# Forget sums and token counts kept on VectorE's side in the first pass of a gated two-layer kernel

## The reference

```python
log_f = log_sigmoid(fg)                       # per head
cs = concat([0, cumsum(log_f)])
log_d = where(tri, (cs - cs.T)[1:, 1:] + ig.T, neg)
m = max(log_d, axis=-1)
d = exp(log_d - m)
c = q @ (k.T / sqrt(dh)) * d
n = maximum(sum(c), exp(-m))
h = c / (n + eps) @ v
...
idx = argmax(softmax(x @ wg))                 # one expert of 8 for each token
mask1 = one_hot(idx)
locations1 = cumsum(mask1, axis=0) - 1.0      # a token's place in its expert's queue
```

## Time and profile before

| what | value |
|---|---|
| median of three runs | 575.7 us (573.4 to 580.27) |
| the profiled execution | 577.31 us, its span 575.5 us |
| so outside the span | 1.8 us |
| first pass | about 0 to 285 us of the span |
| from the gate products at 50.68 us to those at 228.75 us | 12 steps, 14.8 us each on average |
| mean granted clock of TensorE over the span | 0.848 |

### The profile page before, as it was taken

The page is one execution under the profiler, slowest core; times in us unless marked ns, Lnnn a source line. Parts: engine busy times, 40 slices in busy tenths (PEclk is TensorE's granted clock), DMA queues, the critical chain, the costliest instruction groups (busy, mean ns, idle before and its releaser), DMA issues. The chain is left out here.

```text
span 575.5 us, 12773 instructions
## 1 busy us (share of the span) xinstructions
PE 478.4 (83%) x3787; PEld 358.4 (62%) x3787; DVE 333.2 (58%) x1455; ACT 306.5 (53%) x764; POOL 217.1 (38%) x210
## 2 busy tenths in 40 slices
PE   3589999999999999964469999999905788888884
PEld 2567787887877778843327777777702455665652
DVE  6335778877778777796322223333213667788772
ACT  4667666656566656331123333333204678888872
POOL 4301124434444435456500000000058888888400
PEclk9997778777787777795569999999965999999997
DMA  4973112222222111141122443343142556666531
GB/s 120 211 197 92 57 57 75 76 75 74 74 75 74 55 54 38 29 122 37 38 55 56 110 111 110 110 109 93 38 113 34 111 109 145 142 137 139 132 93 36
DMA packets 85067, 51.98 MB, mean 90 GB/s; under 512 B 7555, under 2 KB 78886, under 8 KB 85030
## 3 DMA queue, kind: packets, MB, share of 16 engines
q1 hardware_dynamic: 73766, 43.09, 27.3%
q0 software_dynamic: 11264, 8.43, 8.6%
HBM read 26.07 MB, written 16.91 MB: 75 GB/s over the span
## 5 line engine op out<-in xcount | busy, mean ns | idle before, releaser
L684 POOL DMA_INDIRECT s_xs<-slots_y,s_gidx x64 | 98.8, 1544 | 153.8 <-DMA slots_y<-s_ye 134.6
L814 ACT ACTIVATE s_ht<-heads,s_cols 128x512 f32<-128x512 f32 x64 | 44.0, 687 | 85.0 <-PE heads L1061 84.7
L147 ACT ACTIVATE s_xn<-s_xs,s_ln_shift,s_ln_rstd 128x128 f32 (+1 forms) x192 | 77.6, 481 | 15.6 <-DVE s_ln_shift L140 15.5
L662 POOL DMA_INDIRECT slots_x<-s_xn,s_sidx x64 | 62.8, 982 | 22.9 <-issue 22.9
L99 DVE BATCH_NORM_STATS2 s_ln_stats<-s_xs 128x6 f32 (+1 forms) x256 | 54.5, 279 | 25.8 <-DMA s_xs<-slots_y,s_gidx 20.3
L1061 PE MATMUL heads<-s_xet,s_w_sb 128*128 128x512 f32 x128 | 60.2, 615 | 1.7 <-DVE s_xet L1433 1.7
L1068 PE MATMUL bank<-s_w_sb,s_ht 128*128 128x128 f32 x512 | 59.9, 276 | 0.9 <-DVE s_ye L1442 0.9
L1068 PEld LDWEIGHTS bank<-s_w_sb,s_ht 128*128 128x128 f32 x512 | 58.5, 192 | 1.5 <-issue 1.5
L648 POOL TENSOR_TENSOR s_hs<-s_hs,s_head_w 128x512 f32<-128x512 f32 x16 | 20.3, 1268 | 95.0 <-DVE s_hs L1314 94.9
L960 PE MATMUL heads<-s_dec_r,s_dec_l 128*128 128x512 f32 x64 | 50.6, 938 | 2.0 <-DMA s_dec_r<-s_mrow 2.0
L985 PE MATMUL heads<-s_vaug,s_cw 64*64 64x33 f32 x1024 | 50.1, 270 | 0.1
(11 more groups left out here) (190 smaller groups left out, 934.5 us busy)
## 6 DMA issues: line engine op xcount, KB each, us to landing
slots_x<-s_xe SPq DMA_DIRECT2D x8, 516.0 KB, 8.2
s_xe<-slots_x SPq DMA_DIRECT2D x16, 258.0 KB, 3.0
s_xs<-in_x_dram SPq DMA_DIRECT2D x16, 256.0 KB, 3.0
s_ctxb<-in_ctx_dram SPq DMA_DIRECT2D x16, 256.0 KB, 3.2
s_kpt<-s_kt SPq DMA_DIRECT2D x16, 256.0 KB, 2.8
s_w_sb<-in_L_ffn_w_dram SPq DMA_DIRECT2D x16, 256.0 KB, 3.2
slots_y<-s_ye SPq DMA_DIRECT2D x16, 256.0 KB, 2.3
s_ctxv<-in_ctx_dram SPq DMA_DIRECT2D x16, 256.0 KB, 3.7
```

What stands on the lines that cost most here:

```text
L147: last = act.activation(out(t), tile(t), ACT.Identity, bias=self.shift[:, j:j + 1], scale=self.rstd[:, j:j + 1])
L662: pool.indirect_dma_start(out=slots_x, out_offset=bass.IndirectOffsetOnAxis(ap=sidx[:, q, t:t + 1], axis=0), in_=xn2[:, q, t, :], in_offse ...
L684: pool.indirect_dma_start(out=xs[:, n * D:(n + 1) * D], out_offset=None, in_=slots_y, in_offset=bass.IndirectOffsetOnAxis(ap=gidx[:, n:n + ...
L814: act.activation(ht[:, s_par, c, :], heads[:, c, :], ACT.Gelu_apprx_tanh, bias=col).then_inc(h_done, 1)
```

## The change

Two narrow float32 products leave the PE's list, and DVE takes over what they added.

Maxima: a_values also copies the forget sums from PSUM to SBUF (`fsum`, on the same engine behind the subtraction), and turn_a waits for this copy. turn_maxima keeps only the product with the identity. A new DVE call, token_maxima, adds `fsum` to the turned maxima and writes `mtok`; it stands between the two halves of decayed_scores. exp_m reads `mtok` from SBUF. gate_products, which waited for exp_m (`em_done`), now waits for token_maxima (`mtok_done`), since that is now the reader of bank 6.

Counts: the carried counts are kept on all 128 partitions (`upto`). find_places adds them to the 40 columns of the product in one operation, and multiplies by the one-hot choice afterwards, so the second waits for the first. The single-row product and one constant of POOL are gone (29 setup steps in place of 30).

```diff
             def exp_m(g, half, q):
-                act.wait_ge(mt_ps, g + 1)
+                act.wait_ge(mtok_done, g + 1)
                 need(act, n_done, g - 1)
-                act.activation(em[:, q, :], bank[6][:, 256:256 + R], ACT.Exp, scale=-1.0).then_inc(em_done, 1)
+                act.activation(em[:, q, :], mtok[:, :], ACT.Exp, scale=-1.0).then_inc(em_done, 1)
...
                 pe.wait_ge(kt_done, g + 1)
-                hold(pe, em_done, g, consts)
+                hold(pe, mtok_done, g, consts)
                 pe.wait_ge(qt_done, g + 1)
...
             def turn_a(g, half, q):
-                pe.wait_ge(a_done, g + 1)
+                pe.wait_ge(fsum_done, g + 1)
...
                 hold(pe, mrow_done, g + 1, consts)
-                pe.matmul(bank[6][:, 256:256 + R], tri[:, :], logf[:, :], start=True, stop=False)
-                pe.matmul(bank[6][:, 256:256 + R], mrow[:, q, :], ident[0:R, 0:R], start=False, stop=True).then_inc(mt_ps, 1)
+                pe.matmul(bank[6][:, 256:256 + R], mrow[:, q, :], ident[0:R, 0:R], start=True, stop=True).then_inc(mt_ps, 1)
...
                 for t in range(GT):
-                    pe.matmul(cum[:, (t + 1) * E:W], ones_b[:, :],
-                              onehot[:, t:t + 1, :].to_broadcast([P, GT - t, E]), start=False, stop=False)
-                pe.matmul(cum, ones_f[:, :], carry[:, q:q + 1, :].to_broadcast([1, GT + 1, E]),
-                          start=False, stop=True).then_inc(cum_ps, 1)
+                    last = pe.matmul(cum[:, (t + 1) * E:W], ones_b[:, :],
+                                     onehot[:, t:t + 1, :].to_broadcast([P, GT - t, E]), start=False, stop=(t == GT - 1))
+                last.then_inc(cum_ps, 1)
...
                 dve.wait_ge(gate_act, nth(g, 2, 2))
-                need(dve, mt_ps, g)
+                need(dve, f_ps, g)
...
                 dve.tensor_tensor(am[:, q, :], gates[:, 0, :], bank[6][:, 64:64 + R], ALU.subtract).then_inc(a_done, 1)
+                dve.tensor_copy(fsum[:, :], bank[6][:, 64:64 + R]).then_inc(fsum_done, 1)
...
+            def token_maxima(g, half, q):
+                dve.wait_ge(mt_ps, g + 1)
+                need(dve, em_done, g)
+                hold(dve, fsum_done, g + 1, consts)
+                dve.tensor_tensor(mtok[:, :], bank[6][:, 256:256 + R], fsum[:, :], ALU.add).then_inc(mtok_done, 1)
...
-                dve.tensor_tensor(own[:, :, :], cum[:, 0:GT, :], onehot[:, 0:GT, :], ALU.mult).then_inc(slot_steps, 1)
-                dve.tensor_copy(carry[:, 1 - q, :], cum[0:1, GT, :]).then_inc(cum_used, 1)
+                dve.tensor_tensor(upto[:, q, :, :], cum, upto[:, 1 - q, GT:GT + 1, :].to_broadcast([P, GT + 1, E]),
+                                  ALU.add).then_inc(cum_used, 1)
+                hold(dve, cum_used, g + 1, consts)
+                dve.tensor_tensor(own[:, :, :], upto[:, q, 0:GT, :], onehot[:, 0:GT, :], ALU.mult).then_inc(slot_steps, 1)
...
                 if three:
-                    for u in range(2):
-                        decayed_scores(three[0], three[2], u)
+                    decayed_scores(three[0], three[2], 0)
+                if two:
+                    token_maxima(*two)
+                if three:
+                    decayed_scores(three[0], three[2], 1)
```

More of the change, by code:

```diff
@@ L201, in flamingo @@
         prio_i = sb("prio_i", [P, E], I32)
-        ones_f = sb("ones_f", [1, P])
-        carry = sb("carry", [1, 2, E])
-        carry_i = sb("carry_i", [1, E], I32)
+        upto = sb("upto", [P, 2, GT + 1, E])
+        upto_i = sb("upto_i", [P, E], I32)
         reset = sb("reset", [R, P])
@@ L262, in flamingo @@
         mrow = sb("mrow", [R, 2, P])
+        fsum = sb("fsum", [P, R])
+        mtok = sb("mtok", [P, R])
         em = sb("em", [P, 2, R])
@@ L345, in flamingo @@
         mt_ps = sem("mt_ps")
+        fsum_done = sem("fsum_done")
+        mtok_done = sem("mtok_done")
         em_done = sem("em_done")
@@ L432, in one_row @@
             return v.rearrange("(a n) -> a n", a=1)
-        IDENT_AT, ROWS_AT, TRI_AT, CONSTS = 2, 5, 7, 30
+        IDENT_AT, ROWS_AT, TRI_AT, CONSTS = 2, 5, 7, 29
         block = ctx.enter_context(nc.Block())
@@ L637, in _ @@
             step(pool.iota(prio_i[:, :], pattern=[[-1, E]], base=E, channel_multiplier=0))
-            step(pool.memset(ones_f[:, :], 1.0))
             step(pool.memset(nsq_bias[:, :], 1e-9))
-            step(pool.iota(carry_i[:, :], pattern=[[N, E]], base=-1, channel_multiplier=0))
+            step(pool.iota(upto_i[:, :], pattern=[[N, E]], base=-1, channel_multiplier=0))
             step(pool.tensor_copy(prio[:, :], prio_i[:, :]))
-            step(pool.tensor_copy(carry[:, 0, :], carry_i[:, :]))
+            step(pool.tensor_copy(upto[:, 1, GT, :], upto_i[:, :]))
             assert done == CONSTS
@@ L1085, in _ @@
             need(pe, hs_done, NG)
-            need(pe, em_done, NG)
+            need(pe, mtok_done, NG)
             turn_slots(0, 0, 0)
```

## The result

The changed kernel takes 601.84 us (median of 4, 599.14 to 606.84), the kernel before on the same chip 577.99 us: ratio 1.0431, 95% interval 1.0379 to 1.0484. It is slower by 24 us. The profiled execution took 606.84 us, the longest of the four, with a span of 605.1 us; so the profile shows 29.6 us more span than the one before, some 6 us more than the medians do.

What follows compares the result with a forecast made beforehand. The prediction took the bound to be a circle in which PE and DVE wait for each other; 577.3 + 17.9 - 0.9 + 0.5 + 4.8 = 599.6, said as 600 us, with an 8 in 10 range of 588 to 612.

Steps and rivals of the forecast that it cites:

- The wait put in: Ahead of the gate products: PE waits for DVE's new sum, 1.38 us a step over 13 steps, 17.9 us.
- Products removed save nothing: Two products off PE's list: their 0.64 us a step lie where PE now waits anyway, so no gain.
- The clock: Gate products to forget_sums: the clock falls earlier, six of twelve stretches slow in place of three, adding 4.8 us.
- Given back at the second norm: PE's wait for the second norm's rows at line 993: 0.9 us in all, subtracted from the sum.
- The tail and the start: Last steps of the first pass: DVE's added dependent operation may show, 0 to 1.2 us, taken as 0.5.
- the loaded steps: Sign, full steps of the first pass: they take 16 to 17 us in place of 14.8.
- PE was busy: Sign, first pass between 60 and 240 us: PE's busy share falls below 92%.
- The wait ahead of the gate products: Sign: PE idles 1.5 to 2.5 us per loaded step before the first gate product, 20 to 28 us in all.
- DVE's wait for forget_sums: Sign, first pass: DVE's wait for the product of forget_sums stays near 2 us a step.
- the clock staying low in all stretches: Rival, gate products to forget_sums: every one of twelve stretches takes 11.1 us, total 609 us; chance 0.2.
- PE setting the pace: Rival, first pass: PE's shorter list counts, 16 x 0.64 = 10 us gained, total 567 us; chance 0.05.
- The delay given back by the clock: Rival, gate products to forget_sums: all twelve stretches take 8.5 us, 16 us less, total 579 us; chance 0.07.

Runs made afterwards that it cites:

- e2: Kernel before, with only a wait added: gate_products also waits for the first half of the decayed scores; 601.4 us, ratio 1.036.
- e1: Changed kernel with DVE's new sum (token_maxima) moved to right behind the choice, ahead of the Newton steps and heads; 585.1 us, ratio 1.011.
- e3: Kernel before with only the counts half of the change (carried counts on all partitions, single-row product gone); 579.5 us, ratio 1.001.
- e6: Kernel before plus seven 512-column products, results unused, right ahead of the gate products; 567.3 us, ratio 0.978.
- e9: Changed kernel with the counts half undone, so only the maxima half of the change remains; 600.7 us, ratio 1.034.
- e4: Changed kernel plus seven 512-column products, results unused, right ahead of the gate products; 578.2 us, ratio 0.997.
- e10: Kernel before plus 512-column products, results unused: four ahead of the gate products, three between them and the head values; 596.2 us, ratio 1.025.
- e7: Changed kernel plus 36 products of 16 columns, results unused, ahead of the gate products; 599.5 us, ratio 1.038.
- e8: e1 plus 512-column products, results unused, three ahead of the gate products and three behind them; median 576.2 us, executions 567.1 to 592.6 us.

## Why the prediction was right

**The wait put in**: 1.38 us a step, 17.9 us. Measured: "ahead" went from 4.96 to 6.27 us, 13 x 1.31 = 17.0 us. The parts agree as well. The gate products come 1.01 to 1.02 us behind the start of the decayed scores in eight steps and 0.86 us in five, 0.96 on average (I had 0.98, and 0.10 for the copy, 1.08 in all). The decayed scores come 0.05 us later behind forget_sums on average (5.31 against 5.26). One part is made up of other pieces than I said: the sum ends 0.76 us behind the start of the decayed scores (171.77 to 172.53), not 0.88, and from there to the gate products it is 0.26 us, not 0.10. e2 shows this wait to be the cause, e1 that it goes with the place of the sum.

**Products removed save nothing**: right, but my reason covered only half. I said that they lie in the idle time before the gate products. e1 and e3 show that they are worth nothing without the new wait either, since PE then waits for the choice. My figure of 10 us for the case that PE sets the pace was thus no possible gain, and the 4.4 us expected of e3 fell with it.

**The clock**: 4.8 us, six of twelve stretches at 11 us. Measured in the profiled execution: in the same twelve steps nine took 10.8 to 11.8 us and three 9.5; "behind" grew by 0.79 us, 13 x 0.79 = 10.3 us. The term is mis-sized: 4.8 us forecast, 10.3 measured, and 11.2 if the 0.9 us below, which lie in the same stretches, were given back. That the profiled execution, the slowest of four, had more of it than the others is likely but not shown; e9 and e2, with nearly the same wait, have 10.1 and 10.3 us behind. That the fall comes ahead of the gate products more often was right (four of twelve, none before). What I had named as the cause, idle time, is not the whole of it: e6 raises the clock where there is next to no idle time.

**Given back at the second norm**, -0.9 us: PE's wait at line 994 is no longer among the waits of the changed kernel, as forecast. **The tail and the start**: 0.5 us forecast. The gate products of the fourth group come 2.1 us later, 1.0 of it the first such wait and 1.1 from the steps before, where PE waited 3.7 us in place of 2.0 for the DMA of the maxima; what is left of the span behind the last forget_sums is 1.3 us longer. No run tells these two from chance: in e6, with the tail of the kernel before, the time from the last forget_sums to the last counts is 44.0 us against 41.5 before, more than either.

Sum of the measured terms: 17.0 + 10.3 + 1.1 + 1.3 = 29.7 us for 29.6 us of span. It has to come out, since the last term is what the others leave; it is no proof of them. The prediction had 22.3 us over its profiled execution, the medians say 23.9, and the two profiled executions are 29.5 us apart. So there was some luck in the number: 600 us is 2 us from the median, but the sum was worked out on a profiled execution, and against the profiled one (606.84) it is 7 us short, most of it by the clock. The mechanism, the wait at the place of the sum, is right and rightly sized.

Of the signs that I named, the loaded steps took 17.0 us ((257.06 - 52.82) / 12; forecast 16 to 17) and PE was busy for 157.8 of the 180 us from 60 to 240, 88% (forecast below 92%). The wait ahead of the gate products is 21.8 us over the whole first pass (15.1 put down to the sum, 6.7 to "issue"), forecast 20 to 28. DVE's wait for forget_sums rose to 2.5 us a step, where I had "near 2". From the experts' first products on, the span is 282.9 us against 282.1.

**The rivals**: the clock staying low in all stretches came nearer than its 0.2 suggested (nine of twelve). PE setting the pace is refuted, even in e1. The delay given back by the clock did not occur by itself; e4 forces it, and then the time is that of the kernel before. That rival had worked out 579 us, from other parts: it had 8.5 us for every stretch and no filler, and e4 has 7.5 us on average and a longer "ahead".

## What to carry to other kernels

A busy share of 98% does not say that an engine sets the pace: look for who waits for it and for whom it waits, and take the distance from one to the other on the timeline. When work moves to another engine, its price is its place in that engine's queue, not its length: 0.16 us of work that could have started 1.7 us earlier and stood behind other work cost 1.3 us a step here, and moved ahead of that work it took three quarters of the loss with it. And where the granted clock of TensorE is well below 1 in a stage that is busy throughout, a few wide products whose results nobody uses are worth a run, even where there is hardly any idle time to put them in (here 2% on the kernel before). It takes several executions, since number and place decide between a gain (e6, 0.978) and a loss (e10, 1.025).

## What the runs showed of the hardware

Seven products of 512 columns a step raised the granted clock between 60 and 220 us from 0.75 to 0.90 in the kernel before (e6), where PE was busy for 156.5 of the 160 us already. In the changed kernel they raised it from 0.71 to 0.90 (e4), and 36 products of 16 columns in their place only to 0.75 (e7), at the same busy share. The size of it was new to me as well: the stretch behind the gate products takes 6.3 us at 2.4 GHz throughout (e4) and 9.5 us, at a mean of 0.64, in most steps of the kernel before. Three such products on either side of the gate products gave 567 us in two executions and 585 and 593 us in two others of one kernel (e8), a spread that no other kernel here showed. Four and three gave a clock of 0.80 and a loss (e10).
